# Order of two groups of DMAs on SyncE, and reader-less products on TensorE, in an adaLN attention and MLP block

## The reference, cut to what matters

```
h    = layernorm(x) * (1 + ca) + sa
q,k,v = h @ w_qkv.T, 16 heads of 8 features
attn = q.k * 8**-0.5, minus the row's maximum
p    = stablemax3(attn)              # 1 / cubic(-attn), divided by its row sum
x1   = x + ga * (p @ v @ w_out.T + b_out)
h2   = layernorm(x1) * (1 + cb) + sb
out  = x1 + gb * MLP(h2)             # 128(x2) -> 512 -> 512 -> 128, weights +1 or -1, relu
```

## Time and profile before

| | |
|---|---|
| median of 3 runs | 770.63 us (767.33 to 777.27) |
| profiled execution, span of its trace | 768.64 us, 766.8 us |
| PE, DVE, ACT, POOL busy | 644.4, 631.9, 598.2, 596.3 us (84, 82, 78, 78% of the span) |
| mean granted TensorE clock | 0.924 of full |
| SP: DMAs L971 (rows of maxima), L982 (gathers) | 256 of 2 KB, 128 of 32 KB |

### The profile page before, as it was taken

How to read it: one execution, slowest core, us unless ns; L and a number is a source line. 1 busy time by engine, 2 the same in 40 slices (tenths; PEclk the granted TensorE clock), 3 DMA queues, 4 the chain that set the end, 5 groups by cost and what they waited for, 6 DMA issues and landing times.

```text
span 766.8 us, 9627 instructions
## 1 busy us (share of the span) xinstructions
PE 644.4 (84%) x2993; PEld 250.1 (33%) x2993; DVE 631.9 (82%) x778; ACT 598.2 (78%) x555; POOL 596.3 (78%) x404
## 2 busy tenths in 40 slices
PE   5466768767789899989999898989898999888887
PEld 3122212212222342234322342335233433252264
DVE  6789998988899799989998999989997999844010
ACT  2037787986898889988998899789997899859621
POOL 6129787888889797999889988989797888876410
PEclk9555786978999999999999999999999999979999
DMA  4414113331124113411333113411341131001000
GB/s 146 136 57 151 43 50 84 102 106 50 44 62 152 39 49 101 160 49 50 93 95 121 48 37 88 159 31 48 86 159 49 50 88 50 8 11 42 15 18 14
DMA packets 43670, 56.36 MB, mean 73 GB/s; under 512 B 11436, under 2 KB 27076, under 8 KB 43620
## 3 DMA queue, kind: packets, MB, share of 16 engines
q1 hardware_dynamic: 42948, 54.44, 23.5%
q10 hardware_dynamic: 672, 1.31, 0.5%
HBM read 32.06 MB, written 18.89 MB: 66 GB/s over the span
## 4 chain that ended last, share of the span: by engine, by line
PE 40%; DVE 24%; ACT 15%; issue 14%; SPq 3%; DMA 2%; ACTq 0%; POOL 0%; DVEq 0%; POOLq 0%
DVE mx L719 12%; DVE cub L710 10%; PE OP L498 9%; ACT sq L537 7%; PE MB L423 6%; PE SA L481 6%; PE Z L466 5%; ACT prob L548 5%; PE MB L433 3%; PE SA L423 2%; SPq L971 2%; ACT hid L591 2%; PE MB L404 1%; PE MB L405 1%; PE MB L398 1%
## 5 line engine op out<-in xcount | busy, mean ns | idle before, releaser
L836 POOL TENSOR_TENSOR cub<-cub 128x2048 f32<-128x2048 f32 x128 | 460.3, 3600 | 80.1 <-DVE cub L710 79.4
L537 ACT ACTIVATE sq<-Z,shift 128x1024 f32<-128x1024 f32 x256 | 280.9, 1118 | 81.2 <-PE Z L466 80.1
L710 DVE SCALAR_TENSOR_TENSOR cub<-sq,Z 128x1024 f32<-128x1024 f32 x256 | 310.2, 1213 | 39.3 <-ACT sq L537 39.0
L719 DVE TENSOR_REDUCE mx<-SA 128x2 f32<-128x1024 f32 x248 | 302.1, 1218 | 36.3 <-PE SA L481 32.9
L548 ACT ACTIVATE prob<-cub 128x2048 f32<-128x2048 f32 x128 | 245.0, 1916 | 0.0
L481 PE MATMUL SA<-KH,QL 64*128 64x512 f32 x496 | 128.5, 514 | 52.7 <-DVE mx L719 44.2
L466 PE MATMUL Z<-QH,KH 64*128 64x512 f32 x512 | 134.9, 523 | 32.8 <-DVE cub L710 29.2
L498 PE MATMUL OP<-prob,Vq 128*16 128x512 f32 x1024 | 146.4, 648 | 0.4 <-ACT OT L599 0.4
L466 PEld LDWEIGHTS Z<-QH,KH 64*128 64x128 f32 x512 | 51.1, 195 | 220.5 <-DVE cub L710 138.7
L423 PE MATMUL MB<-hid,W 128*128 128x512 f32 x216 | 119.5, 641 | 0.3 <-ACT hid L591 0.3
L481 PEld LDWEIGHTS SA<-KH,QL 64*128 64x128 f32 x496 | 50.0, 198 | 142.7 <-DVE mx L719 110.5
(11 more groups left out here) (124 smaller groups left out, 433.8 us busy)
## 6 DMA issues: line engine op xcount, KB each, us to landing
parts_q<-SQ SPq DMA_DIRECT2D x32, 256.0 KB, 2.5
QL<-parts_q SPq DMA_DIRECT2D x64, 128.0 KB, 2.5
QH<-parts_q SPq DMA_DIRECT2D x64, 128.0 KB, 2.7
KH<-parts_k SPq DMA_DIRECT2D x62, 128.0 KB, 2.6
parts_k<-SK SPq DMA_DIRECT2D x28, 256.0 KB, 2.7
QH<-mp SPq DMA_DIRECT2D x256, 2.0 KB
nd<-OT SPq DMA_DIRECT2D x128, 32.0 KB
xa<-L_attn_x SPq DMA_DIRECT2D x8, 256.0 KB, 3.7
```

The costliest lines, as they stand in the source:

```text
L537: nc.scalar.activation(sq[:, h, :], Z[:, h, :], ACT.Square, bias=shift[:, 0:1]).then_inc(s_sq, 1)
L710: nc.vector.scalar_tensor_tensor(cub[:, m % RING, h, :], sq[:, h, :], CUB_ADD, Z[:, h, :], ALU.add, ALU.mult).then_inc(s_cv, 1)
L719: nc.vector.tensor_reduce(to, unit_bank(m, u)[:, :, :], AX_X, ALU.max).then_inc(s_mx, 1)
L836: nc.gpsimd.tensor_tensor(ff, ff, ff, ALU.mult).then_inc(s_fp, 1)
```

## The change

In `sp_step` the four gathers of sums are issued ahead of the eight DMAs with the rows of maxima. In `pe_step` a function `fill` is called between the second unit of the logits and the product with V. In 26 steps, which the table `FILL` names, it multiplies one 128x512 piece of the MLP's weights by the identity into MB, and nothing reads the result. It waits until the product that was in MB last has been copied out (`s_taken`) and for the weights (`s_wts`). Behind the last batch, in b = 8, the copy of l1_3 on ScalarE moves behind "den_sq" and "den_inv", which move from n = 6 to n = 5.

```diff
 MISC[B] = [
-    ("l1_1", -2, [(0, "c", 2), (1, "d", 2)]), ("l1_2", -2, [(4, "d", 4)]), ("l1_3", -2, [(5, "c", 4)]),
+    ("l1_1", -2, [(0, "c", 2), (1, "d", 2)]), ("l1_2", -2, [(4, "d", 4)]), ("l1_3", -2, [(5, "d", 4)]),
...
+FILL = {(FIRST, n): ("v", 1) for n in range(13, 16)}
+FILL |= {(0, n): ("k", 2) for n in range(2, 13)} | {(0, n): ("v", 2) for n in (14, 15)}
+FILL |= {(1, n): ("k", 3) for n in range(2, 8)} | {(1, n): ("x1", 1) for n in range(9, 13)}
...
-AT[B] = MAIN_AT | {"w2g": 2, "st2": 8, "mv2": 8, "rs2": 9, "x1n": 9}
+AT[B] = MAIN_AT | {"den_sq": 5, "den_inv": 5, "w2g": 2, "st2": 8, "mv2": 8, "rs2": 9, "x1n": 9}
...
+            def fill():
+                if (b, n) in FILL:
+                    name, count = FILL[b, n]
+                    pe.wait_ge(s_taken[name], count)
+                    pe.wait_ge(s_wts, 1)
+                    nc.tensor.matmul(MB[:, :], ident[:, :], W1[:, n % KC, :], start=True, stop=True)
...
             logits(m, 1)
+            fill()
             with_v(s)
...
+            quad, tb = (s - 1 - AV_BEHIND) // QUAD, (s - 1 - AV_BEHIND) % QUAD
+            if 0 <= quad < B * NQ and tb == TB - 1:
+                beta, g = quad // NQ, quad % NQ
+                sp.wait_ge(s_ot, quad + 1)
+                if g == 0:
+                    need(sp, s_made["x1"], beta)
+                for j in range(QUAD):
+                    r = 32 * g + HD * j
+                    sp.dma_start(nd[r:r + HD, :, :], OT[32 * j:32 * j + 2 * HD, quad % 2, :]).then_inc(s_gat[quad % 2], 16)
+
             if (s + AHEAD - 4) % QUAD == 0 and 0 <= s + AHEAD - 4 < GROUPS:
...
-            quad, tb = (s - 1 - AV_BEHIND) // QUAD, (s - 1 - AV_BEHIND) % QUAD
...
```

## The result

The changed kernel took 743.87 us (median of 4 runs, 740.32 to 745.58) against 768.98 (4 runs, 763.43 to 777.27): a ratio of 0.969, 95% interval 0.962 to 0.976. It is faster by some 25 us; 747 had been forecast, 22 us off. Every ratio leaves out executions that are over 1.5% longer than the fastest of their kernel. Its profiled execution took 743.44 us, with a span of 741.6.

A forecast was written before the change was run, and what follows sets the result against it. VectorE was taken as the bound, working 18.74 of 19.57 us in an ordinary quad. Terms of 14.0 + 1.2 + 3.6 + 3.5 = 22.3 us off 768.64 gave 746.3, forecast as 747, range 738 to 758.

The forecast's parts named there:

- The gathers: Quads with den_sq, batches 1 to 7: gathers issued earlier end ScalarE's wait, 14.0 us off (bounds 7.0 and 17.9).
- the clock after the stalls: Gather quads of batches 2 and 7: less low TensorE clock behind the stall, 1.2 us off (bounds 0 and 4.5).
- The rows of maxima: Eight DMAs now behind the gathers: still there 1.7 us before the scores in n = 1 and n = 5, cost 0.
- The end: Last batch: den_sq 2.37 us earlier, no idle time or low clock around x1, 3.6 us off (bounds 2.4 and 4.2).
- The fillers: 26 products without a reader: 4.0 us off in batches 0 and 1, 0.5 back, 3.5 net.
- at full clock 0.89 + 1.05 = 1.94 fits and hides: Steps with V: filler and product with V fit within VectorE's two instructions of 2.3 us; at half clock 1.3 late.
- one of the prediction's own signs of being wrong: Steps with a filler: the prediction would be wrong if VectorE waited in them; no size given.
- the clock stay over 0.95: From n = 5 of batch 0 on: sign that the fillers work, with batches 0 and 1 shorter by 4 us.
- the 6.2 us to be had: Four quads of batches 0 and 1: idle time the fillers may give back, mostly counted above 0.83 us; 4.0 taken.
- Rival 1: Batches 0 and 1: fillers give nothing, 3.5 to 5 us missing, 751 us; chance 0.20.
- rival 3: Steps with V at half clock: each of 20 fillers delays the scores by 1.3 us, 777 us; chance 0.04.

The follow-up runs named there:

- e3: Kernel before with only the end changed: den_sq and den_inv in n = 5, ahead of the copy of l1_3; 766.08 us, ratio 1.000.
- e1: Kernel before with only the four gathers moved ahead of the rows of maxima on SyncE; 748.96 us, ratio 0.975.
- e2: Kernel before with only the 26 products without a reader added, ahead of the product with V; 766.26 us, ratio 0.999.
- e10: Kernel before with only the 26 products without a reader added, at the end of the step; 758.05 us, ratio 0.986.
- e11: Changed kernel with the fillers at the end of the step and the end of the program as before the change; 737.08 us, ratio 0.957.
- e4: Changed kernel without its 26 products without a reader; 745.22 us, ratio 0.971.
- e8: Changed kernel with the 26 products without a reader moved to the end of the step, behind the next step's first logits; 733.26 us, ratio 0.957.

## Why the prediction was right, and where its terms were not

**The gathers: right in the mechanism, short in size.** ScalarE's waits are gone, and the quad of batch 3 came out at 20.43 us (20.7 forecast). The seven quads gave 21.0 us, where 14.0 for the stall and 1.2 for the clock behind it had been taken. Both terms were too small. The stall is 2.1 us on VectorE in batches 2 to 5, as read from batch 3, but more in the last two. In batch 6 VectorE waited 3.0 us for the square. The quad of batch 6 before, then in e3 with the stall at full clock, then after:

```profile
571.04:595.29 24.25, 20.51 (x96) 7.97 (x92) 18.66 (x20) 18.53 (x19) 19.33 (x15) 0.93 0.16 48
572.73:595.36 22.63, 18.94 (x96) 7.07 (x92) 18.64 (x20) 18.53 (x19) 19.29 (x15) 1.00 0.15 44
558.73:578.60 19.87, 18.78 (x96) 7.08 (x92) 18.64 (x21) 18.42 (x19) 19.21 (x15) 1.00 0.17 48
```

So the stall was worth 2.8 us there and the low clock 1.6. In batch 7 VectorE's wait for the square went from 2.8 to 0.2. That makes about 16 us for the seven stalls, an estimate (five at 2.1, 2.8 and 2.6).

The term that was mis-sized most is the clock after the stalls: 1.2 us was taken "since it is partly chance", within bounds of 0 and 4.5, and it was the rest of the 21.0, about 5. It is 1.5 us in batch 2, 1.6 in batch 6 and some 2 in batch 7; no run has the stall of batch 7 at full clock, so that this last split is not shown. Batch 6 was left out of the term altogether, though its quad is as long before as that of batch 2. Chance was the right word for where the low clock comes, the wrong one for how much: with the stall gone no execution that was profiled had low clock in these quads of batches 2 to 6.

**The rows of maxima: right.** The cover of 1.7 us was forecast; nothing waited, 1 us more cost nothing, 2.4 more cost 15.7 us.

**The end: the wait right, the clock behind it by luck.** 3.6 us were forecast, 2.4 for the wait and 1.2 since "without the stall that should not happen"; 3.8 were measured by the two traces, 2.5 and 1.3. But y does not always slow down behind this wait. From the start of x1 to the end it took 36.9 us in the kernel before and 38.2 in e1, and 35.5 to 35.6 in e2, e10 and e11, which have the same 2.73 us of idle time, as in the kernels without it. So 2.5 us are there each time, and the 1.3 only in some executions, the profiled one of the kernel before among them. Why e3 gained nothing that could be measured is open: its trace gained 2.5 us from the last mp on, and had 1.9 us more in the nine quads up to batch 2 than that of the kernel before, with the same work.

**The fillers: wrong in two steps.** The first: "at full clock 0.89 + 1.05 = 1.94 fits and hides". It does not hide: at full clock each cost 0.2 to 0.4 us, and at half clock, where 1.3 was worked out for a step with 1.7 for the filler, the filler took 2.07 and VectorE stood for 1.83. I had compared the two products with VectorE's two instructions alone. But the scores behind them feed ScalarE's square first, and in the changed kernel VectorE waited for that square at full clock, and for the logits at half clock. That VectorE would wait in steps with a filler was one of the prediction's own signs of being wrong; nor did the clock stay over 0.95 from n = 5 of batch 0 on (0.92 in three quads). The second: the 6.2 us to be had were counted down to the 0.83 us of idle time of a quad with MLP work. That was no floor: without those products VectorE's idle time goes to 0.00, and the fillers at their right place gave some 12 us (745.22 to 733.26; 12.5 over the nine quads of the traces). Forecast 3.5; measured 0.2 in the eight quads of the two traces, and 1.4 by the medians of e4 and the change, neither to be told from nothing. Rival 1, that the fillers give nothing, came true in that part, without its 751, since the gathers gave more. (The mean clock of the four quads that rival 3 names is 0.76 and not 0.77; nothing hangs on it.)

The total lies in the range of 738 to 758 and came out near the forecast by luck: forecast 22.3 us off, measured 25.1. The stalls and the clock behind them gave 5.8 us more than was taken, and the fillers 3.3 less, by the traces.

**Best version.** e8, gathers first, the end as changed, fillers at the end of the step: 733.26 us in the median, 0.957 of the kernel before.

## What to carry to other kernels

A stall costs its own length on the bounding engine, and in some executions again what the clock does behind it: look for low clock behind every instance of a stall before sizing its removal, and size each instance by itself. Work that exists only to hold the clock up is a queue entry like any other: put it where nothing that another engine waits for stands behind it, which here was worth some 12 us, against 1.4 or nothing. And take the floor of a bounding engine's idle time from its own busy time, not from a stretch that carries other work.

## What the runs showed of the hardware

- The same stall of 2.1 us on VectorE was followed by a clock of 0.93 in the quad in batch 2 and not in batches 3 to 5 of one execution, and in batches 2 and 4 of another. Such a quad took 1.5 us more (24.12 against 22.57). In batch 6 the low clock cost 1.6 us in one execution (0.93) and was absent in another.
- Behind the same 2.73 us of idle time of TensorE at the end of the program, the first records of y took 1.91 and 1.92 us in two executions (the kernel before and e1) and 1.06 in three (e2, e10, e11).
- A product that nothing reads, of 128x512 in float32 with 128 rows, took 2.07 us at half clock and 1.12 at full clock.
- Four gathers of 32 KB, SBUF to SBUF, were there 1.8 us after SyncE had issued the last; the eight DMAs of 2 KB, 1.1 us after the earlier trace rows. SyncE spent 0.72 us on issuing one of the former and 0.55 on one of the latter (2.88 us for four, 4.44 for eight).
